# Attention B: the positive and the negative part of k and q formed by ScalarE with Relu instead of VectorE with max and min

## What is computed

```python
def _sigma(x):
    return jax.nn.elu(x) + 1.0
def step(carry, qkv):                       # one segment of 64 tokens, 16 heads of 8
    M, z = carry
    q, k, v = qkv
    sq = _sigma(q)
    A_mem = jnp.matmul(sq, M) / (jnp.sum(sq * z[:, :, None, :], axis=-1, keepdims=True) + EPS)
    scores = jnp.where(causal, -jnp.inf, jnp.matmul(q, jnp.swapaxes(k, -2, -1)) * inv_sqrt_dk)
    A_dot = jnp.matmul(jax.nn.softmax(scores, axis=-1), v)
    A_s = beta * A_mem + (1.0 - beta) * A_dot
    sk = _sigma(k)
    V_prev = jnp.matmul(sk, M) / (jnp.sum(sk * z[:, :, None, :], axis=-1, keepdims=True) + EPS)
    return (M + einsum('bhtk,bhtv->bhkv', sk, v - V_prev), z + jnp.sum(sk, axis=-2)), A_s
```

## Time and profile before

| | |
|---|---|
| median of 3 runs | 1674.24 us (1666.82 to 1677.94) |
| profiled execution | 1675.07 us, span 1673.3 us |
| TensorE busy | 1459.9 us (87%) |
| VectorE busy | 1220.1 us (73%) |
| ScalarE busy | 869.2 us (52%) |
| GpSimd busy | 902.9 us (54%) |

### The profile page before, as it was taken

How to read it: one execution, slowest core, us unless ns; L and a number is a source line. 1 busy time by engine, 2 the same in 40 slices (tenths; PEclk the granted TensorE clock), 3 DMA queues, 4 the chain that set the end, 5 groups by cost and what they waited for, 6 DMA issues and landing times. The chain is left out here.

```text
span 1673.3 us, 46472 instructions
## 1 busy us (share of the span) xinstructions
PE 1459.9 (87%) x13668; PEld 1242.3 (74%) x13668; DVE 1220.1 (73%) x3362; ACT 869.2 (52%) x2019; POOL 902.9 (54%) x1308
## 2 busy tenths in 40 slices
PE   5899999999999999997587738999999999999986
PEld 3899889898889898897366526766676766667665
DVE  4378888888888888886245446888888888878774
ACT  2466666666666666665366623444444444444431
POOL 4456666666666666664588833444444444444431
PEclk9899999999999999999699958999999999999996
DMA  4423333233333232330444223333333333333330
GB/s 138 147 76 100 94 94 85 78 81 85 94 94 83 78 84 85 91 87 11 118 123 133 84 75 96 102 102 101 107 103 101 108 106 107 107 106 107 98 96 17
DMA packets 181695, 158.10 MB, mean 94 GB/s; under 512 B 12530, under 2 KB 163186, under 8 KB 181619
## 3 DMA queue, kind: packets, MB, share of 16 engines
q1 hardware_dynamic: 181618, 157.17, 32.9%
HBM read 113.09 MB, written 44.04 MB: 94 GB/s over the span
## 5 line engine op out<-in xcount | busy, mean ns | idle before, releaser
L597 PE MATMUL a_bank<-a_vp,a_prob 128*128 128x74 f32 x4096 | 603.6, 253 | 0.0
L597 PEld LDWEIGHTS a_bank<-a_vp,a_prob 128*128 128x128 f32 x4096 | 588.6, 192 | 7.5
L685 DVE TENSOR_REDUCE a_nmax<-a_bank 128x2 f32<-128x512 f32 x512 | 345.7, 681 | 142.9 <-PE a_bank L566 142.0
L484 ACT ACTIVATE a_prob<-a_bank 128x512 f32<-128x512 f32 x512 | 305.4, 596 | 245.8 <-PE a_bank L581 240.5
L581 PE MATMUL a_bank<-a_q_st,a_k_st 120*128 120x256 bf16 x1024 | 281.7, 276 | 27.6 <-POOL a_q_st L345 27.0
L566 PE MATMUL a_bank<-a_k_st,a_q_st 96*128 96x256 bf16 x1024 | 259.9, 277 | 16.9 <-DVE a_nmax L685 12.5
L1627 PE MATMUL c_o_bank<-c_vb,c_prob 128*128 128x96 f32 x1024 | 173.4, 293 | 17.9 <-DVE c_ad L1910 14.0
L1786 DVE TENSOR_REDUCE c_nmax<-c_bank 128x4 f32<-128x512 f32 x256 | 164.8, 684 | 19.7 <-PE c_bank L1597 17.2
L345 POOL TENSOR_SCALAR a_q_st<-a_mt 24x2048 bf16<-24x2048 bf16 x64 | 121.4, 1896 | 103.7 <-PE a_bank L581 60.8
L1492 ACT ACTIVATE c_prob<-c_bank 128x256 f32<-128x256 f32 x256 | 98.8, 386 | 145.8 <-PE c_bank L1577 144.2
L404 POOL TENSOR_TENSOR a_prod<-a_ov,a_wgt 128x512 f32<-128x512 f32 x128 | 151.3, 1182 | 37.3 <-POOL a_prod L404 17.1
(11 more groups left out here) (207 smaller groups left out, 2879.3 us busy)
## 6 DMA issues: line engine op xcount, KB each, us to landing
a_q_st<-scratch_a_parts_dram SPq DMA_DIRECT2D x64, 288.0 KB
a_k_st<-scratch_a_parts_dram SPq DMA_DIRECT2D x192, 96.0 KB
c_q_st<-scratch_c_parts_dram SPq DMA_DIRECT2D x64, 288.0 KB
c_k_st<-scratch_c_parts_dram SPq DMA_DIRECT2D x192, 96.0 KB
scratch_a_parts_dram<-a_parts SPq DMA_DIRECT2D x32, 384.0 KB, 2.7
scratch_c_parts_dram<-c_parts SPq DMA_DIRECT2D x32, 384.0 KB, 2.7
a_x<-in_x SPq DMA_DIRECT2D x32, 128.0 KB, 2.9
scratch_y<-a_y SPq DMA_DIRECT2D x32, 128.0 KB, 2.5
```

Source lines behind the costliest of these rows:

```text
L484: act.activation(prob[h % 4][:, :, :].rearrange("p a b -> p (a b)"), t_ps[h % 2][:, :], ACT.Exp).then_inc(exped, 1)
L597: mm = pe.matmul(o_ps[g % 2][:, at:at + VM], prob[h % 4][:, c, t * P:(t + 1) * P], vp[o][:, c, 0:VM], start=c == 0, stop=c == NT - 1)
L685: dve.tensor_reduce(nmax[:, t, 2 * g:2 * g + 2, 0], s_ps[t][:, :].rearrange("p (h k) -> p h k", h=2), AX.X, ALU.max, negate=True).then_inc ...
```

## The change

DVE's two instructions of step 1, max(x, 0) and min(x, 0), go. ScalarE gets two in step 2: Relu(x), and Relu(-x) by a scale of -1. The second is the negative part with its sign turned, and so the exponential takes it with a scale of -1. Both read the same bank as before. DVE waited for `kq_d`. ScalarE needs no such wait, since it made `kq` itself. The wait for `sg_d` (the buffers are free) moves along.

```diff
@@ scalar engine, body @@
                         act.mul(skn[SEG:P, 1:NS - 1, :].rearrange("p s f -> p (s f)"),
                                 ps_c[0:SEG, P:(NS - 1) * P], -1.0).then_inc(sk_d, 1)
+                    if s == 2 and active(j, u, 0):
+                        if later(j, n, 1):
+                            act.wait_ge(sg_d, n)
+                        act.activation(flat(pos), ps_a[:, :], ACT.Relu).then_inc(pn_d, 1)
+                        act.activation(flat(neg), ps_a[:, :], ACT.Relu, scale=-1.0).then_inc(pn_d, 1)
...
                         act.wait_ge(pn_d, (n + 1) * 2)
                         if later(j, n, 1):
                             act.wait_ge(sg_d, n)
-                        act.activation(nexp[:, :, :], neg[:, :, :], ACT.Exp).then_inc(nexp_d, 1)
+                        act.activation(nexp[:, :, :], neg[:, :, :], ACT.Exp, scale=-1.0).then_inc(nexp_d, 1)
@@ vector engine, body @@
-                    if s == 1 and active(j, u, 0):
-                        dve.wait_ge(kq_d, (n + 1) * 2)
-                        if later(j, n, 1):
-                            dve.wait_ge(sg_d, n)
-                        dve.tensor_scalar(flat(pos), ps_a[:, :], 0.0, None, ALU.max).then_inc(pn_d, 1)
-                        dve.tensor_scalar(flat(neg), ps_a[:, :], 0.0, None, ALU.min).then_inc(pn_d, 1)
```

## The result

The changed kernel takes 1691.83 us in the median (1690.12 to 1693.94, 4 runs), the kernel before 1673.33 us beside it. The ratio is 1.0106 with a 95% interval of 1.0082 to 1.0130. The profiled execution has a span of 1689.3 us.

The account below looks back on a forecast made before the run. TensorE, 91% busy, was taken as nearly the bound, its idle time being winnable. DVE's 0.99 us gain, cut to 0.82 by GpSimd, times 30 bodies gave 25 us: 1650 us, 1.5% faster, range 1640 to 1664.

Parts of the forecast that it names:

- what GpSimd takes back: Step 4: z4 waits 0.40 us for GpSimd's root of the variance, cutting the body's gain from 0.99 to 0.82 us.
- `mpart` comes at 1313.06 - 0.99 = 1312.07: At TensorE's L1698: DVE delivers mpart 0.99 us earlier and still decides there, with 0.27 us of waiting left.
- The gain of 0.99 us at the reductions of step 2: DVE, without pos and neg, starts the first score reduction at 1307.62 instead of 1308.61.
- L1657's wait gone: TensorE's wait for am: L1657 starts 0.78 us earlier, all of its idle time in that body.
- ScalarE's hole: The 2.04 us after step 2's exponential; two Relu passes, estimated at 1.2 us, fit there and delay nothing.
- the free scale: The scale of -1 in ScalarE's exponential is priced at nothing, being a field of the same instruction.
- the transfer: Rival: loads of q_st and k_st for step 1's L1594 become the bound; no change, 1674 us; chance 0.09.
- The sum, 25 us: Whole loop of attention B: 30 bodies times 0.82 us gained, giving 1650 us, 1.5% faster; chance 0.57.
- the forecast's upper end of 0.99: Rival, per body of the loop: DVE's gain with nothing taken back, 31 us in all, 1644 us; chance 0.12.
- a case slower than before, by TensorE's clock: Rival: TensorE's 95% share costs the full clock, 12 us more per affected body; six give 1721 us; chance 0.06.
- The case in which the gain stops at GpSimd: Rival: a body gains only about 0.5 us, 15 us in all, 1659 us; chance 0.16.
- the 0.25 us of cover: DVE's old wait for a score before step 4's reduction, expected to absorb part of z4's delay, leaving 0.81 us gain.

Follow-up runs that it names:

- sum_after_norm: The changed kernel plus one wait: GpSimd adds pos and nexp to sg only after DVE has written both halves of z4; 1655.44 us, ratio 0.9899.
- overlap_before: The kernel before plus a useless GpSimd sum (kq + kq into rest) per body at the time of z4; 1694.89 us, ratio 1.0147.

## Why the prediction was wrong

**The step that failed** is in the part on what GpSimd takes back: "The reduction behind it starts at about 1312.98 + 0.59 = 1313.57." The 0.59 us is a duration of `z4` from a body in which nothing ran beside it. I had moved `z4` to 1312.98, and the same text moves `nexp` forward through ScalarE by 0.78 us. I never wrote down where that puts GpSimd's sum, which follows `nexp`: 1314.25 - 0.78 = 1313.47, 0.12 us before the forecast end of `z4`, 1313.59. `z4` then came 0.40 us later than I had it, and the sum was ahead of it by 0.02 us. The measured distance from the start of `z4` to the start of the reduction is 1.94 us, not 0.59. sum_after_norm and overlap_before show the cause from both sides: take the sum away from `z4` and it is fast in the changed kernel, bring one to it and it is slow in the kernel before.

**What it cost.** The reduction of step 4 was to start 0.81 us earlier than before and started 0.94 us later, 1.75 us off. Of this 1.35 us are `z4`'s length. The other 0.40 us are its later start: GpSimd's variance began 0.44 us behind the splits and not 0.18 (0.26 us), and `z4` began 0.20 us behind the root and not 0.06 (0.14 us). The 0.06 was given without a row. The 0.18 was read between splits, and why the variance waits longer no run shows. In sum_after_norm these 0.40 us remain (on the same zero `z4` starts at 1313.37), and a body gains 0.57 us and not the forecast 0.82. That is the size of the miss that is left without the hold: 1.0% and not 1.5%.

**The cast.** "`mpart` comes at 1313.06 - 0.99 = 1312.07" was 0.41 us early. 0.32 of these are the cast held by the fourth split, the same mechanism again. The rest stays open.

**What held.** The gain of 0.99 us at the reductions of step 2 (measured 0.98), L1657's wait gone (0.89 us earlier, forecast 0.78), the Relu passes at 0.62 and 0.63 us in ScalarE's hole with 1.06 us left over, one table load, the free scale, the transfer with room to spare and a granted clock of 1.00 in the loop. The sum, 25 us, was too high even without the hold of `z4`: sum_after_norm gains about 17 us (1.0%). Only where `z4` has left DVE, so that neither the hold nor the wait for the root is there, is the change worth 0.98 us a body, the forecast's upper end of 0.99.

**The rivals.** I had a case slower than before, by TensorE's clock, and the kernel was slower by something else. The case in which the gain stops at GpSimd named the right place, "three engines meet within 0.3 us", and took it for a matter of cover only. It also asked what happens if the 0.25 us of cover isn't there, but not what happens if two engines are at work at the same time. The rule that I weighed, relu belongs on VectorE (the Trainium skill, page "ScalarE: Activation LUTs", section "Rules for kernel authors"), had no bearing: ScalarE's passes cost nothing that the runs can tell.

The rule that did bear on it I left unused. The Trainium skill, page "SBUF — State Buffer", section "Who interferes with whom", says that DVE shares its second pair of SBUF ports with GpSimd. A DVE instruction in one of the fast two-port modes (tensor_scalar, copy and cast can be in one), or one with two SBUF inputs beside a GpSimd instruction that reads SBUF, excludes GpSimd and is excluded by it, and the one that issues first keeps the ports to its end. A reduction never contends there. The runs agree on which forms are held: `z4` as tensor_scalar and as scalar_tensor_tensor (2.01 and 2.14 us a pair), the cast (0.49 us) and, beside a split, the subtraction with two SBUF inputs (up to 0.39 us). `z4` was also held by a memset that only writes, and the reduction was not held (0.17 us). On who comes first the traces can't settle it: as tensor_scalar `z4` started 0.05 to 0.06 us ahead of GpSimd's instruction in two kernels and was held, as scalar_tensor_tensor it started 0.07 us ahead and held GpSimd's sum. With the 1.35 us that the overlap measured, the forecast's 0.82 us gained would have been about 0.5 us lost a body.

## What to carry to other kernels

When a change moves work in time, write down where every neighbour on DVE and GpSimd goes, and look for pairs that now lie side by side and didn't before: a duration read from a trace is valid for the company in which it was measured. Here an instruction that was two to four times longer with the same shape was in a conflict, and the row on the other engine that ended less than 0.1 us before it was the cause. Look at the single instructions: a row that sums two of them hid the memset's hold. Test a change that lost with the collision removed before you drop it: one wait on an engine that wasn't critical turned 1.1% slower into 1.0% faster here.

## What the runs showed of the hardware that I had not expected

- DVE and GpSimd exclude each other on SBUF. A DVE tensor_scalar of 128 x 128 f32 took 345 ns alone and 1328 ns behind a 1.27 us sum of GpSimd; a cast of 128 x 16 took 0.49 instead of 0.17 us behind a split.
- The form of the instruction decides: the same cast written as a reduction over an axis of one took 0.17 us beside the same split. The hold then fell in part on the next instruction with two SBUF inputs, 0.17 to 0.39 us.
- A lead of 0.05 to 0.06 us by the trace doesn't protect `z4`: it was held with GpSimd's sum starting at 1299.10 and `z4` at 1299.04, as well as with the sum at 1320.17 and `z4` at 1320.19. In the kernel before it was safe, done 0.11 us before the sum.
- A GpSimd instruction that only writes holds DVE too. Beside a memset of 0.52 us the first half of `z4` took 0.65 us instead of 0.34 and ended 0.08 us behind it.
- The hold goes both ways: GpSimd's sum took 1.40 instead of 1.27 us when `z4` as scalar_tensor_tensor had started 0.07 us ahead of it.
